# Gathers in groups of four, with a wait for a group's landing between two groups

## What is computed

```python
s, idx = jax.lax.top_k(sub_scores, K)
all_scores = (s[:, :, 0, :, None] + s[:, :, 1, None, :]).reshape(-1, H, K * K)
all_idx = (idx[:, :, 0, :, None] * E + idx[:, :, 1, None, :]).reshape(-1, H, K * K)
best_s, best_pos = jax.lax.top_k(all_scores, K)
indices = jnp.take_along_axis(all_idx, best_pos, axis=-1)
w_down = w_down_embed[indices]
w_up = w_up_embed[indices]
x = jnp.einsum('nd,nhkd->nhk', q_tok, w_down)
x = jax.nn.gelu(x)
vals = x * jax.nn.softmax(best_s, axis=-1)
out = jnp.einsum('nhk,nhkd->nd', vals, w_up)
```

## Time and profile before

| | |
|---|---|
| time, median of 3 runs | 3447.02 us (3434.35 to 3462.33) |
| profiled execution, its span | 5577.0 us |
| granted TensorE clock, mean of the span | 0.719 |
| PE busy | 3254.3 us (58%) |
| DVE busy | 2619.7 us (47%) |
| ACT busy | 2226.7 us (40%) |
| POOL busy | 2330.6 us (42%) |
| gathers, queue q0 | 316.15 MB, 20.5% of 16 DMA engines |
| queue q10 / q1 | 130.06 MB, 7.5% / 69.45 MB, 4.2% |

### The profile page before, as it was taken

One profiled execution on the slowest core, in us unless ns is written; L12 is line 12 of the kernel. 1 busy time (PEld: TensorE's weight loads), 2 busy tenths in 40 slices (PEclk: granted clock), 3 DMA queues, 4 the chain that ended last, 5 costly groups with the idle time before them and its releaser, 6 DMA issues. The chain is left out here.

```text
span 5577.0 us, 53095 instructions
## 1 busy us (share of the span) xinstructions
PE 3254.3 (58%) x14195; PEld 2193.0 (39%) x14195; DVE 2619.7 (47%) x13857; ACT 2226.7 (40%) x4627; POOL 2330.6 (42%) x2451
## 2 busy tenths in 40 slices
PE   4356445556665554655655665656546655665678
PEld 2133233334334333443433434434333433443456
DVE  3443554544454445444543554554435445544633
ACT  2235232234543442344425433543534344344444
POOL 4544444353443444434344434443353444444410
PEclk7556677676777776787767777777767777776879
DMA  5223224142332432243233324333332333343320
GB/s 172 89 80 105 69 81 136 55 118 78 99 95 71 121 91 81 78 120 102 77 101 96 93 76 116 91 90 104 105 90 68 102 97 99 90 116 91 95 79 3
DMA packets 314967, 519.04 MB, mean 93 GB/s; under 512 B 56746, under 2 KB 171308, under 8 KB 314668
## 3 DMA queue, kind: packets, MB, share of 16 engines
q0 software_dynamic: 119808, 316.15, 20.5%
q10 hardware_dynamic: 86784, 130.06, 7.5%
q1 hardware_dynamic: 108076, 69.45, 4.2%
HBM read 498.64 MB, written 11.17 MB: 91 GB/s over the span
## 5 line engine op out<-in xcount | busy, mean ns | idle before, releaser
L766 POOL DMA_INDIRECT ring<-in_table_dram,idx x2432 | 2328.4, 957 | 3015.7 <-PE bank_u L861 1521.4
L1023 PE MATMUL bank_x<-z3t,w_b 128*128 128x255 f32 (+1 forms) x1264 | 425.7, 470 | 410.9 <-ACT eo L3302 194.0
L5409 DVE CUSTOM_DVE_ANT_0 ring<-ring,bank_q 128x128 f32<-128x128 f32 (+1 forms) x2432 | 537.4, 281 | 232.6 <-issue 176.4
L861 PE MATMUL bank_u<-ring,ident 128*128 128x512 f32 (+1 forms) x912 | 543.6, 743 | 151.7 <-ACT ring L3196 66.8
L3196 ACT ACTIVATE ring<-ring,vu 128x128 f32<-128x128 f32 (+1 forms) x1824 | 555.5, 390 | 131.5 <-DVE vu L5415 73.6
L3297 ACT ACTIVATE ht<-bank_x,b_s 128x255 f32<-128x255 f32 (+1 forms) x704 | 289.3, 463 | 657.6 <-remote 404.3
L1026 PE MATMUL bank_x<-ht,w_b 128*128 128x255 f32 (+1 forms) x1264 | 386.7, 459 | 207.5 <-ACT ht L3297 179.3
L1023 PEld LDWEIGHTS bank_x<-z3t,w_b 128*128 128x128 f32 x1264 | 269.4, 236 | 518.0 <-ACT eo L3302 211.8
L1026 PEld LDWEIGHTS bank_x<-ht,w_b 128*128 128x128 f32 x1264 | 283.6, 239 | 295.4 <-ACT ht L3297 197.9
L861 PEld LDWEIGHTS bank_u<-ring,ident 128*128 128x128 f32 (+1 forms) x912 | 206.3, 239 | 392.8 <-issue 280.6
L1070 PE MATMUL bank_x<-qd,tb 128*128 128x128 f32 x1280 | 227.1, 332 | 210.1 <-ACT gs L3227 100.9
(11 more groups left out here) (235 smaller groups left out, 5418.1 us busy)
## 6 DMA issues: line engine op xcount, KB each, us to landing
w_b<-in_w_dram ACTq DMA_DIRECT2D x304, 256.0 KB
ring<-in_table_dram,idx POOLq DMA_INDIRECT x2432
tb<-turned ACTq DMA_DIRECT2D x120, 256.0 KB
tb<-in_table_dram SPq DMA_DIRECT2D x120, 256.0 KB
tb<-turned SPq DMA_DIRECT2D x40, 256.0 KB
tb<-in_table_dram ACTq DMA_DIRECT2D x40, 256.0 KB
gs<-in_table_dram SPq DMA_DIRECT2D x32, 256.0 KB
turned<-gs ACTq DMA_DIRECT2D x32, 256.0 KB
```

The costliest lines, as they stand in the source:

```text
L766: pool.indirect_dma_start(ring[0:rows, u, k, :], None, table, bass.IndirectOffsetOnAxis(ap=idx[0:rows, j, c:c + 1], axis=0)).then_inc(gath ...
L861: ins = mm(U[0:rows, :], ident[0:rows, 0:rows], ring[0:rows, u, 4 * c:4 * c + 4, D:ROW], start=(u == 0 and c == 0), stop=(u == UNITS - 1 a ...
L1023: ins = mm(to[:, m * n:m * n + n], wa[:, k * D:(k + 1) * D], x, start=True, stop=True)
L5409: ins = dve.tensor_tensor_reduce(w, w, qrep[r, b, :], 1.0, 0.0, ALU.mult, ALU.add, xu[r, k:k + 1])
```

## The change

Within a unit, POOL now waits before the fifth, ninth and thirteenth gather, until all gathers of this unit so far have landed. The last group of a unit is followed by the next unit's first with no wait of this kind between them.

```diff
                     for k in range(UR):
                         c = u * UR + k
+                        if k % 4 == 0 and k:
+                            pool.wait_ge(gathered[u], (t * UR + k) * 16)
                         pool.indirect_dma_start(
                             ring[0:rows, u, k, :], None, table,
                             bass.IndirectOffsetOnAxis(ap=idx[0:rows, j, c:c + 1], axis=0)).then_inc(gathered[u], 16)
```

## The result

| | before | after |
|---|---|---|
| time, median | 3447.05 us (3434.35 to 3462.33, 4 runs) | 4363.41 us (4359.5 to 4365.96, 4 runs) |
| ratio, 95% interval | | 1.2653 [1.2615, 1.2691] |
| profiled execution, span | 5577.0 us | 4357.6 us |
| TensorE clock, mean | 0.719 | 0.797 |

The kernel became 27% slower, 916 us. The forecast was 4250 us, between 3650 and 4530. The profiled execution of the changed kernel lasts as long as its timed ones, unlike that of before. All times and ratios here are of fast executions; one slow one, 4529 us at a granted clock of 0.545 in the kernel with fewer gathers and waits, is left out.

A forecast was written before the change was run, and what follows sets the result against it. The prediction took POOL's issue of gathers as the bound: a floor of 3345 us plus 866 us for 456 waits gives 4211, and with 40 us of old waits left 4250 us, range 3650 to 4530.

The forecast's parts named there:

- The direction and the mechanism: Slower, chance 0.85: POOL, bound by issuing gathers, stands at each of 456 new waits until the gather before has landed.
- Its signs: POOL idles about 1000 us in 456 named waits, its wait for unit sums shrinks far below 1521 us, gathers stay 0.95 us.
- The floor: Least time of the timed kernel before: 58 us head, 3057 us of POOL issuing 2432 gathers, 230 us tail, 3345 us.
- Bound by POOL, the others close behind: Timed kernel before: POOL's issue of gathers sets the time, 97% of 3447 us, with the other engines near it.
- The reading of the long profile: In the 5577 us execution long gather bursts nearly stop the other engines; grouping lets its span fall towards 4200 to 4700.
- the timed runs cannot contain much of that: Stops of other engines: even without them TensorE would need 3784 us and VectorE 3540 us, more than the timed runs.
- The price of a wait: Each new POOL wait: landing 1.6 plus waking 0.6 less usual gap 0.3, 1.9 us; 866 us for 456.
- The landing at the loaded start: First unit's 16th gather: VectorE's dots start 5.5 us after its end; not believed for the mean wait.
- The cover: New waits cost nothing where POOL waited anyway: of 102 us of old waits, 40 stay.
- POOL with slack: Rival, chance 0.24: the 0.30 us gap between gathers may be the profiler's; 3550 to 4050 us, or about no change.
- No change: Rival: POOL's new waits find their data landed, or the whole gap is slack; about 3450 us, chance 0.03 + 0.03.
- Faster: Rival, chance 0.09: long bursts partly stop other engines in timed runs too, groups of four end it; about 3300 us.

The follow-up runs named there:

- the kernel with fewer gathers and waits: Changed kernel with two of each unit's sixteen gathers left out from the third tile on: 4013.61 us, ratio to the kernel before 1.164.
- the pause experiment: Kernel before with ten small chained POOL memsets at each place where the change puts a wait, looking at no landing: 4147.21 us, ratio 1.2001.
- The second profile of before: Kernel before, unedited, profiled once more: span 3437.4 us.

## Why the prediction was right or wrong

**The direction and the mechanism: right.** The waits stand on POOL's issue path, and nothing hides them. The chain of the changed kernel and the pause experiment show it. Its signs came: 455 waits named for the landings, 1171.6 us for about 1000; 2.2 us left of the wait for the unit sums; a gather of 0.967 us in the mean.

**The floor: right in size, by two errors that partly cancel.** 3345 us were worked out from gathers at 1.257 us, the head of 58 us and a tail of 230 us. The second profile of before has 3437.4 us less 80.1 us of waits, and with the usual gap in their place 3362 us: a pitch of 0.979 + 0.305 = 1.284 us, 66 us more, and a tail of 181 us, 49 less.

**"Bound by POOL, the others close behind": half right.** They are not behind but about level: with fewer gathers the time stays. For this change it made little difference; for one that speeds POOL up it would have been a wrong forecast of 360 us.

**The reading of the long profile: wrong in its cause.** The step "the timed runs cannot contain much of that" came to a right end and saved the forecast, but one of its two numbers doesn't hold. It used TensorE's busy time of the long execution, 3254 us; with the 2848.7 us of the second profile it gives 2848.7/0.86 = 3313 us, less than the timed 3447. And the stop was not a thing of long bursts: with bursts unbroken it is gone, in three kernels. That the profiled span fell to 4357.6 us, in 4200 to 4700 as forecast, was luck, as a second profile of before falls without any grouping. The gathers' timing in the earlier trace rows, which the sum used, was sound even in that execution.

**The price of a wait: mis-sized in the landing.** Forecast 1.6 + 0.6 - 0.3 = 1.9 us, measured 2.57 - 0.30 = 2.27 us. By the prediction's own sign, an idle of 1.9 to 2.4 us and near 2.1, the landing was wrong. The 1.6 us of the earlier trace rows are the time until the last data moved. The same time in the changed kernel is 1.95 us in the mean, and there 0.35 of the 0.37 us of the error lie. The count on the semaphore is full another 0.40 us later, which the prediction had no term for; but its 0.6 us for waking covers what follows the last data, 2.57 - 1.95 = 0.62 us. That it fits is luck: the 0.8 us of the earlier trace rows behind a sum of TensorE held another path, and what the counting instruction has in them no run shows. With the experts' loads made light a wait was 0.13 us shorter, so sharing with them is an estimated 0.13 us of the 0.35; the rest is open. The landing at the loaded start, 5.5 us in the earlier trace rows, stands at the far end (longest wait 7.0 us). By the page of the Trainium skill that the prediction cited (DMA: Bandwidth & Descriptors, Anatomy of one DMA), a landing would be an estimated 2.3 us from a gather's start; measured from there it is 0.97 + 2.31 = 3.28 us, so the page's figure would have been further off than the row.

**The cover: 62 us forecast as swallowed, about 115 measured.** Between the second profile of before and the changed kernel the new waits add 1035 us. From that go 77 us of old waits (41 named, 35 under "issue"), which is the cover that the prediction meant and a little more than its 62, 30 us of quicker gathers (2381.9 to 2352.3 us busy) and 9 us of tail; 920 remain, the difference of the spans. That a gather gets a little quicker was no term of the sum; that the less dense other engines are the reason is not shown.

Together, against 4250: the price adds 456 x 0.37 = 169 us, the greater cover takes 53 away and the base of 3437 us in place of 3447 takes 10, which gives 4356 for a span of 4357.6.

**The rivals.** POOL with slack: refuted, 152 waits cost 242 us, and in the changed kernel a gather counts 1.21 us. The upper end of its range, 4050 us, doesn't follow from the prices either: half the gap with the dearest is 2980 + 1186 = 4166. No change: would have needed landings within 0.3 us. Faster: refuted with its ground, since the timed runs have no stop to be relieved of and the pitch is not under 1.0 us.

## What to carry to other kernels

A wait for a DMA just issued costs its whole landing on the issuing engine (here 2.3 us beside a pitch of 1.27 us), while a wait for one that is in already costs nothing: whoever wants to bound what is in flight should wait for landings that are some gathers back (here at least four). A landing is over when the semaphore has its count, not when the last data have moved. When a profiled execution is far longer than the timed ones, take a second one before explaining its shape; single durations in it may still hold, its idle time doesn't. In a list of waits, look also at the long gaps that it can't name: here they were half of all. And before work is taken from the engine at the bound, ask whether another one is level with it: here most of what was added on POOL counted (0.74 of it with one wait a unit, 0.89 with three), and next to nothing of what was taken away.

## What the runs showed of the hardware

- One execution of the kernel before took 5577 us; in the later part of eight bursts TensorE was busy in 44.1 and VectorE in 39.0 of 217 us, while the gathers kept their pitch of 1.25 us. The next profiled one took 3437 us. The cause is open.
- POOL starts a gather 0.26 us after the full count of the landing that it waited for in the two pieces shown, 0.23 us in the mean, shorter than the 0.30 us between two gathers in a row.
- In the changed kernel the semaphore has its full count 0.40 us in the mean after the gather's last packet.
- A landing takes 2.31 us in the mean from the end of the gather's instruction, and about as long behind two gathers (2.52 - 0.26 = 2.26) as behind eight (2.68 - 0.26 = 2.42).
- A wait that is already met leaves the gap between two gathers at 0.30 us, at 452 of 453 places.
